# The second layer's matrix on one core: rotated rows of a scaled matrix against an elementwise product with a broadcast row of scales

## What is computed

```python
def L0(x):  return unit_rows((adj @ x + x) @ w0 + b0)
def L1(h):                                   # 5 gated steps
    for _ in range(5):
        m = adj @ h                          # both halves of av are the same here
        z, r = sigmoid(av @ w3.T + h @ u3.T + ...), sigmoid(av @ w4.T + h @ u3.T + ...)
        h = (1 - z) * h + z * tanh(av @ w5.T + (r * h) @ u5.T + ...)
def L2(x):                                   # the layer whose matrix the change is about
    A_hat = adj + eye(512)
    d = sum(A_hat, axis=-1) ** -0.5
    return (d[:, None] * A_hat * d[None, :]) @ x @ W.T + b
def L3(x):  A = softmax(masked values); return (A * eye) @ h0 + (A * (1 - eye)) @ h1 + bias
x = layernorm(x + L(x))                      # after each of the four
```

## Time and profile before

| | us |
|---|---|
| median of 3 runs | 772.51 |
| lowest and highest run | 772.34, 774.0 |
| the profiled execution, its time | 772.56 |
| its span, first to last instruction | 770.8 |

### The profile page before, as it was taken

How to read it: one execution, slowest core, us unless ns; L and a number is a source line. 1 busy time by engine, 2 the same in 40 slices (tenths; PEclk the granted TensorE clock), 3 DMA queues, 4 the chain that set the end, 5 groups by cost and what they waited for, 6 DMA issues and landing times.

```text
span 770.8 us, 11992 instructions
## 1 busy us (share of the span) xinstructions
PE 751.6 (98%) x3788; PEld 630.0 (82%) x3788; DVE 620.5 (81%) x1431; ACT 519.8 (67%) x1088; POOL 162.9 (21%) x314
## 2 busy tenths in 40 slices
PE   8999999999999999999999999999999999799996
PEld 6888788888888888888888888888887887688885
DVE  5899998888888877887777777777999999775553
ACT  4799877666667766666666666665687789954334
POOL 1778420000000000000000000000123268653334
PEclk9999999999999999999999999999999999999999
DMA  7500000000030001000000000000000000000112
GB/s 224 203 1 2 1 1 1 1 1 1 0 117 1 1 5 51 1 0 1 1 1 0 0 0 0 0 0 2 1 1 1 1 2 1 3 12 28 56 56 83
DMA packets 9894, 16.60 MB, mean 22 GB/s; under 512 B 2928, under 2 KB 4464, under 8 KB 9200
## 3 DMA queue, kind: packets, MB, share of 16 engines
q1 hardware_dynamic: 9840, 15.94, 6.0%
HBM read 8.59 MB, written 5.24 MB: 18 GB/s over the span
## 4 chain that ended last, share of the span: by engine, by line
PE 83%; ACT 9%; DVE 5%; issue 2%; DMA 1%; POOL 0%; SPq 0%; ACTq 0%; DVEq 0%
PE agg_ps L963 13%; PE agg_ps L965 13%; PE agg_ps L964 13%; PE gate_ps L899 7%; PE gate_ps L901 7%; PE gate_ps L900 7%; PE cand_ps L899 4%; PE cand_ps L901 4%; PE cand_ps L900 4%; PE turn_ps L1002 4%; ACT res L420 3%; PE gate_ps L906 3%; PE cand_ps L906 2%; ACT feat L497 1%; PE turn_ps L1006 1%
## 5 line engine op out<-in xcount | busy, mean ns | idle before, releaser
L963 PE MATMUL agg_ps<-adj_hi,nat_hi 128*128 128x512 f32 x384 | 152.1, 396 | 1.8 <-DVE adj_lo L825 1.8
L965 PE MATMUL agg_ps<-adj_hi,nat_lo 128*128 128x512 f32 x384 | 150.2, 391 | 0.0
L964 PE MATMUL agg_ps<-adj_lo,nat_hi 128*128 128x512 f32 x384 | 149.6, 390 | 0.0
L621 POOL TENSOR_SCALAR shift<-mean_var 128x4 f32<-128x4 f32 x64 | 23.2, 363 | 431.4 <-DVE mean_var L806 428.9
L759 DVE TENSOR_TENSOR agg_lo<-agg_ps,agg_hi 128x512 fp32r<-128x512 f32 x80 | 55.2, 690 | 64.9 <-ACT agg_hi L449 64.9
L482 ACT ACTIVATE reset_hi<-gate_r 128x512 fp32r<-128x512 f32 x80 | 50.6, 633 | 83.3 <-DVE gate_r L776 83.3
L963 PEld LDWEIGHTS agg_ps<-adj_hi,nat_hi 128*128 128x128 f32 x384 | 72.1, 188 | 17.1 <-issue 2.0
L965 PEld LDWEIGHTS agg_ps<-adj_hi,nat_lo 128*128 128x128 f32 x384 | 72.1, 188 | 16.2
L964 PEld LDWEIGHTS agg_ps<-adj_lo,nat_hi 128*128 128x128 f32 x384 | 72.2, 188 | 15.6
L466 ACT ACTIVATE gate_r<-gate_ps,bias 128x512 f32<-128x512 f32 x80 | 55.2, 689 | 43.6 <-PE gate_ps L901 43.5
L449 ACT ACTIVATE agg_hi<-agg_ps 128x512 fp32r<-128x512 f32 x80 | 48.6, 608 | 45.3 <-PE agg_ps L965 45.3
(11 more groups left out here) (181 smaller groups left out, 1792.7 us busy)
## 6 DMA issues: line engine op xcount, KB each, us to landing
res<-in_x SPq DMA_DIRECT2D x16, 256.0 KB, 5.7
out<-res SPq DMA_DIRECT2D x16, 256.0 KB, 2.0
rows<-in_adj SPq DMA_DIRECT2D x4, 256.0 KB, 4.5
adj_hi<-eye_hi SPq DMA_DIRECT2D x1, 1024.0 KB, 9.8
adj_lo<-eye_lo SPq DMA_DIRECT2D x1, 1024.0 KB, 11.6
later<-in_adj SPq DMA_DIRECT2D x1, 1024.0 KB, 6.6
mix_rows<-mix SPq DMA_DIRECT2D x1, 1024.0 KB, 8.1
later<-mix_rows SPq DMA_DIRECT2D x1, 1024.0 KB, 4.9
```

The source lines that it names most:

```text
L963: pe.matmul(ps, nat_hi[:, b, k, :], m_hi[:, k, :], start=(k == 0), stop=False)
L964: pe.matmul(ps, nat_hi[:, b, k, :], m_lo[:, k, :], start=False, stop=False)
L965: last = pe.matmul(ps, nat_lo[:, b, k, :], m_hi[:, k, :], start=False, stop=(k == T - 1))
```

## The change

The matrix is made without TensorE. The transposed adjacency that the steps use is exactly the adjacency once its two parts are added, and scaling both its rows and its columns commutes with transposing. In slots 39 to 42 VectorE adds `adj_hi` and `adj_lo` to `later`, and the identity to the tile's own 128 columns (node `4p+k` stands on partition `p` and in column `k*128+p` of tile `k`). SyncE stores the 512 scales `row_d` to DRAM and loads them back as one row on all partitions (`d_cols`, over a part of `eye_lo` that is free by then). VectorE multiplies tile `k` by that row in slot `42+k`. ScalarE's high part and VectorE's low part, in slots 43 to 46 as before, now read `later` in place of the bank. ScalarE's four scalings, VectorE's diagonal blocks and all rotations of the kind `"l2"` with their diagonal matmuls are gone.

```diff
-SCALE_AT = SUM_AT + 3
-L2_AT = SCALE_AT + 3
+WHOLE_AT = SUM_AT + 2
+L2_AT = WHOLE_AT + T
...
+            sp.wait_ge(row_d_made, 1)
+            sp.dma_start(d_dram[0].rearrange("(t p) -> p t", p=P), row_d[:, :],
+                         allow_slow_non_contiguous=True).then_inc(d_stored, 16)
+            sp.wait_ge(d_stored, 16)
+            sp.wait_ge(turned, TURN_NO["value", T - 1] + 1)
+            sp.dma_start(d_cols[:, :], d_dram[0:1, :].to_broadcast([P, N])).then_inc(d_cols_in, 16)
             sp.wait_ge(mix_stored, 16)
-            sp.wait_ge(turn_read, reads(TURN_NO["l2", T - 1]))
+            sp.wait_ge(l2_lo_made, T)
...
-                for k in range(2 * (s - SCALE_AT), 2 * (s - SCALE_AT) + 2):
-                    if 0 <= k < T:
-                        act.wait_ge(rows_again, 16)
-                        act.wait_ge(row_d_made, 1)
-                        act.activation(later[:, k, :], later[:, k, :], ACT.Copy,
-                                       scale=row_d[:, k:k + 1]).then_inc(rows_scaled, 1)
...
-                    act.activation(eye_hi[:, k, :], turn_ps[n % 2][:, :], ACT.Copy,
+                    act.wait_ge(l2_scaled, k + 1)
+                    act.activation(eye_hi[:, k, :], later[:, k, :], ACT.Copy,
...
-                if s == SCALE_AT:
-                    dve.wait_ge(row_d_made, 1)
-                    dve.wait_ge(turned, TURN_NO["value", T - 1] + 1)
-                    for t in range(T):
-                        last = dve.tensor_scalar(diag_d[:, t * P:(t + 1) * P], ident[:, :], row_d[:, t:t + 1], None, ALU.mult)
-                    last.then_inc(diag_d_made, 1)
+                k = s - WHOLE_AT
+                if 0 <= k < T:
+                    own = slice(k * P, (k + 1) * P)
+                    dve.wait_ge(row_sum_made, T)
+                    dve.tensor_tensor(later[:, k, :], adj_hi[:, k, :].bitcast(F32), adj_lo[:, k, :].bitcast(F32),
+                                      ALU.add).then_inc(l2_whole, 1)
+                    dve.wait_ge(l2_whole, 2 * k + 1)
+                    dve.tensor_tensor(later[:, k, own], later[:, k, own], ident[:, :], ALU.add).then_inc(l2_whole, 1)
...
-                    dve.scalar_tensor_tensor(out=eye_lo[:, k, :], in0=turn_ps[TURN_NO["l2", k] % 2][:, :],
+                    dve.scalar_tensor_tensor(out=eye_lo[:, k, :], in0=later[:, k, :],
                                              scalar=row_d[:, k:k + 1], in1=eye_hi[:, k, :].bitcast(F32), op0=ALU.mult,
-                                             op1=ALU.subtract).then_inc(turn_read, 1)
+                                             op1=ALU.subtract).then_inc(l2_lo_made, 1)
+                k = s - L2_AT + 1
+                if 0 <= k < T:
+                    dve.wait_ge(d_cols_in, 16)
+                    dve.wait_ge(l2_whole, 2 * k + 2)
+                    dve.tensor_tensor(later[:, k, :], later[:, k, :], d_cols[:, :], ALU.mult).then_inc(l2_scaled, 1)
...
-                    elif kind == "l2":
-                        pe.wait_ge(rows_scaled, T)
-                        pe.wait_ge(diag_d_made, 1)
-                        for t in range(T):
-                            cols = slice(t * P, (t + 1) * P)
-                            last = pe.transpose(to[:, cols], later[:, t, i:i + T * (P - 1) + 1:T], ident[:, :])
-                            if t == i:
-                                last = pe.matmul(to[:, cols], ident[:, :], diag_d[:, cols], start=False, stop=True,
-                                                 skip_group_check=True)
```

More of the change, by code:

```diff
@@ L143, in turns_at @@
         found.append(("value", VALUE_AT.index(s)))
-    if L2_AT <= s < L2_AT + T:
-        found.append(("l2", s - L2_AT))
     found += [("result", u) for u in norms_at(s, "turn") if is_step(u)]
@@ L170, in flat, with graph_layers @@
     return v.rearrange("p a n -> p (a n)")
-def graph_layers(nc, x, adj, w0, b0, w3, b3, u3, ub3, w4, b4, w5, b5, u5, ub5, w2, b2, wl3, e, bl3, mix_dram, out):
+def graph_layers(nc, x, adj, w0, b0, w3, b3, u3, ub3, w4, b4, w5, b5, u5, ub5, w2, b2, wl3, e, bl3, mix_dram, d_dram, out):
     with ExitStack() as ctx:
@@ L197, in graph_layers @@
         with ExitStack() as again:
-            _, diag_d = (again.enter_context(nc.sbuf_tensor(n, [P, w], F32)) for n, w in (("above_diag_d", (T - 1) * N), ("diag_d", N)))
+            _, d_cols = (again.enter_context(nc.sbuf_tensor(n, [P, w], F32)) for n, w in (("above_d_cols", (T - 1) * N), ("d_cols", N)))
         eye_lo = sb("eye_lo", [P, T, N], F32R)
@@ L279, in graph_layers @@
         adj_copied, adj_hi_made = sem("adj_copied"), sem("adj_hi_made")
-        row_sum_made, row_d_made, diag_d_made = sem("row_sum_made"), sem("row_d_made"), sem("diag_d_made")
-        rows_again, rows_scaled = sem("rows_again"), sem("rows_scaled")
+        row_sum_made, row_d_made = sem("row_sum_made"), sem("row_d_made")
+        d_stored, d_cols_in = sem("d_stored"), sem("d_cols_in")
+        rows_again = sem("rows_again")
+        l2_whole, l2_scaled, l2_lo_made = sem("l2_whole"), sem("l2_scaled"), sem("l2_lo_made")
         mask_made, neg_made, counted, owner_made = sem("mask_made"), sem("neg_made"), sem("counted"), sem("owner_made")
@@ L547, in slot @@
                     act.wait_ge(mix_stored, 16)
-                    n = TURN_NO["l2", k]
-                    act.wait_ge(turned, n + 1)
-                    act.activation(eye_hi[:, k, :], turn_ps[n % 2][:, :], ACT.Copy,
+                    act.wait_ge(l2_scaled, k + 1)
+                    act.activation(eye_hi[:, k, :], later[:, k, :], ACT.Copy,
                                    scale=row_d[:, k:k + 1]).then_inc(l2_hi_made, 1)
@@ L954, in slot @@
                     if s == AFTER:
-                        pe.wait_ge(turn_read, reads(TURN_NO["l2", T - 1]))
+                        pe.wait_ge(l2_lo_made, T)
                     if s == AFTER + B:
@@ L1072 @@
     args.append(nc.dram_tensor("mix_rows", (N, N), F32, kind="Internal").ap())
+    args.append(nc.dram_tensor("d_cols_row", (1, N), F32, kind="Internal").ap())
     args.append(nc.dram_tensor("out", (B, N, D), F32, kind="ExternalOutput").ap())
```

## The result

The changed kernel takes 770.08 us in the median (769.55 to 773.63, 21 runs), the kernel before in the same runs 773.02 us. The ratio is 0.9968 with a 95% interval from 0.9959 to 0.9977, so the change takes 2.5 us off (1.8 to 3.2). The profiled execution took 770.41 us with a span of 768.5 us, against 772.56 and 770.8 before. The forecast was 769.7 us, in a range of 769.0 to 771.0, with 2.8 us taken off.

The account below looks back on a forecast made before the run. TensorE's own queue was taken to bound this stage. From 772.56 us, 2.80 for the removed loads and 0 for VectorE's new work gave 769.76, or 769.7 us as the median, in a range of 769.0 to 771.0.

Parts of the forecast that it names:

- What bounds the kernel: In the steps' stage TensorE's own work sets the pace; 24 weight loads leaving its queue take off 2.8 us.
- The whole amount reaches the end: Behind the changed slots nothing depends on absolute time, so all 2.8 us should reach the program's end.
- VectorE's cover: Slots 39 to 46: idle time and slack hide VectorE's extras; `agg_lo` may start about 0.78 us late before TensorE feels it.
- Slot 42's extras: VectorE's additions and first multiplication in slot 42: 1.61 us against 1.07 idle, 0.54 us late at most.
- The term that was left open between 0 and 0.24 us: TensorE's loss from VectorE running late in slots 42 to 46; taken as 0.
- the second rival: The l2 rotation covered TensorE's wait for the reset gate; four slots each lose 0.5 us, 771.7 us; chance 0.06.
- some 0.8 us left in the slot: ScalarE's high part, about 0.6 us, fits into the slot shortened by 0.69 us, with about 0.8 us left.
- The queues: The row of scales lands at about 247.5, its reader starts at 259.3; some 11 us to spare.
- VectorE's overrun: VectorE's extras in slots 42 to 45 make TensorE wait for `reset_lo`; between 770.0 and 770.9 us, chance 0.16.
- The fourth rival: The row of scales comes late to VectorE's multiplication ahead of `agg_lo`, making the kernel slower; chance 0.04.
- Its point of decision: Beyond 25.5 + 0.78 us from `row_d`, every further microsecond costs the program one; gain used up at 29.1.

Follow-up runs that it names:

- the removal alone: Kernel before with one 128x128 l2 rotation per slot instead of four and no diagonal matmul; median 771.51 us, ratio 0.9968 to the kernel before.
- the loads put back: Changed kernel with 24 weight loads put back on TensorE as rotations that nobody reads; ratio 0.9999 to the kernel before.
- one more instruction: Changed kernel with one more idle 128x512 VectorE instruction in each of slots 43 to 45; ratio 0.9968 to the kernel before.
- the kernel with six loads: Changed kernel with the row of scales loaded six times, one after the other; ran once, 779.53 us.

## Why the prediction was right, step by step

**What bounds the kernel.** In this stage TensorE's queue, as the earlier trace rows had said: 24 loads fewer took 2.77 us off the window, 2.8 predicted. Both halves of the experiment, the removal alone and the loads put back, gave the sum of the loads to 0.02 us.

**The whole amount reaches the end.** Nearly. The span fell by 2.3 us and not by 2.8. The first difference is at the start, before any changed instruction (first aggregation load before, then after):

```profile
10.63 0.19 PEld L963 LDWEIGHTS agg_ps<-eye_hi,nat_hi 128*128 128x128 f32 x1 [1.32 <-DVE nat_lo L651]
```

```profile
10.86 0.19 PEld L969 LDWEIGHTS agg_ps<-eye_hi,nat_hi 128*128 128x128 f32 x1 [1.65 <-DVE nat_lo L650]
```

That is 0.23 us of the first inputs' arrival, from run to run. The rest, under 0.3 us, lies in the last layer, where VectorE waits 1.6 us for `diag_row` and not 1.3. Its two transfers took 8.3 and 4.8 us where they took 8.1 and 4.7 before, which is those 0.3 us, and in the experiments the first of them landed after anything up to 11.4 us. None of the experiments was made to test either, so that they are scatter is a reading; the median of 21 runs leaves room for it, since its interval holds both 2.3 and 2.8 us. That its value lies so near the forecast's 769.7 us is in part luck: the forecast started from 772.5 us in three runs, and in 21 the kernel before has 773.0.

**VectorE's cover.** Slots 39 to 41 met `agg_lo` with idle times of none, 0.16 and 0.18 us (about 0.1 said). The first came 0.16 us late, which the forecast had not: it took slot 49's idle time of 1.07 us, and the kernel before idles only 0.68 us there. Slot 42's extras took 259.90 - 258.37 = 1.53 us where at most 1.61 was said, and `agg_lo` was 0.37 us late (259.90 against 258.49 + 1.04), not 0.54. In slots 43 to 45 the low part went on after 0.66 us and the multiplication after 0.61, 1.27 where I took 1.31, so each slot gave back about 0.1 us. The term that was left open between 0 and 0.24 us was 0. From the end of `reset_lo` to its load it was 0.48 us at its smallest; where TensorE really waits, 0.06 us of that remain (with one more instruction, 278.64 to 278.70), so about 0.42 us were to spare.

**ScalarE.** The high part took 0.714 us, as the earlier trace rows said, and the reset gate still idled 0.67 us. The update gate's load kept its distance from the reset gate's reading, 268.38 - 268.25 = 0.13 us as in slot 49 before, so the second rival was rightly held small:

```profile
267.56 0.69 ACT L472 ACTIVATE gate_r<-gate_ps,bias 128x512 f32<-128x512 f32 x1 [0.67 <-PE gate_ps L907]
```

```profile
268.38 0.19 PEld L905 LDWEIGHTS gate_ps<-agg_hi,w_hi 128*128 128x128 f32 x1
```

But the argument beside it, some 0.8 us left in the slot, was no cover in itself: 0.89 us more on ScalarE cost 0.49 us per slot through `agg_hi` and VectorE, a way that the forecast did not name.

**The queues.** The store of the scales landed after 7.9 us, the row after 5.4, at 247.4, and its reader started at 259.30: 11.9 us to spare, some 11 said.

**The rivals.** VectorE's overrun did not occur, and where it was forced it cost what its sum says, on the instruction that it names. The Trainium skill's page "VectorE: DVE Perf Modes", section "The DRAIN you can't avoid", says that the next instruction does not start before the pipe is empty, and goes on that one which is not "held" starts earlier. The prediction took the first half alone and found the trace against it. Against the whole it is not: independent instructions start 0.60 to 0.61 us apart at 0.68 to 0.69 us duration, and ten instructions of 0.68 to 0.74 us fit into 6.51 us.

The fourth rival, the late row, was mis-sized. Its point of decision, 25.5 us behind `row_d` and 0.78 more, lies 0.6 us too late, because it sets the reader where `agg_lo` stands, and the reader goes 0.60 us ahead of it. In the kernel with six loads the reader was 263.61 - (259.30 - 0.60) = 4.91 us late and TensorE's load 269.00 - (265.10 - 0.60) = 4.50, so that 0.41 us went unseen (this execution runs 258.49 - 257.89 = 0.60 us ahead of the changed kernel's). And "every further microsecond is one for the program" leaves out the clock: a wait of 4.5 us costs 6.8, one of 6.7 costs 8.7. What waits between 1.4 and 4.5 us would cost at this place was not tried, and the last layer's 2.8 us went either way, so where the gain would have been used up stays open. And its distance was read from landings that are less steady than I took them for: the first store took 7.9 to 8.9 us in the runs, and repeated ones 9.3 to 10.0.

## What to carry to other kernels

Before moving work from the busiest engine to another, count the room in the other's queue as idle time per round plus the slack at the one place where it is waited for; here that sum held to 0.1 us, with the extras of the change and with more. Once the room is used up, the cost goes by the number of rounds, and engines that wait for each other in a circle have a length of their own, which the idle time of one of them does not show. What has plenty of room may still have the worst price when it fails: a late transfer that stopped TensorE for 4.5 us also cost 2.2 us of lower clock behind it.

## What was unexpected in the hardware

- A wait of TensorE of 4.5 us was followed by 4.8 us at a granted clock of 0.50 (1.2 GHz) and cost 2.2 us beyond itself; one of 6.7 us, 2.0 beyond. Waits of 0.9 to 1.4 us, three in a row, left the clock at 1.00.
- The same wait of 2.8 us in the last layer was followed by a granted clock of 1.00 in the kernel before and of 0.50 in the changed one, and nothing in the change touches it. Of nine traces with the changed kernel's last layer and this wait, four show 1.00 in the 3 us behind it and five fall to 0.50. So whether a wait costs the clock is not settled by its length alone here.
- The store of 512 single elements from a 128x4 tile landed after 7.9 to 8.9 us the first time, and after 9.3 to 10.0 when it was repeated.
- The 256 KB row on all partitions landed after 3.9 to 5.4 us the first time, and after 3.0 in the median when it was loaded four times.
